# First attention: the high and low parts of the heads, written to one place each and copied to the second by GpSimd

## The chip, the cores and the metric

The kernel runs on one core of one Trainium2 chip. The metric is device time in microseconds (us), the median over runs of the whole program; before the change it is 892.95 us (three runs, 891.64 to 893.69).

## The reference

The program is a chain of four blocks, each with a residual and a layernorm behind it: polynomial attention, a gated FFN, softmax attention with a relative bias, and a mixture of eight experts with a shared expert. The change lies in the first attention, on x of 8 batches x 256 tokens x 256:

```python
proj = x @ w_qkv
q, k, v = jnp.split(proj, 3, axis=-1)          # 16 heads of 16 columns each
q = apply_rope(q, cos, sin); k = apply_rope(k, cos, sin)
q = layernorm(q, ln_scale, ln_bias)            # over the 16 columns of a head
k = layernorm(k, ln_scale, ln_bias)
a = jnp.einsum('bhnd,bhmd->bhnm', q, k) ** 4
a = jnp.tril(a)
denom = jnp.sum(a, axis=-1, keepdims=True)
out = jnp.einsum('bhnm,bhmd->bhnd', a / denom, v)
out = out.transpose(0, 2, 1, 3).reshape(b, n, e) @ w_out
```

## The kernel before

**Precision.** fp32 values go through TensorE as two numbers of the narrower type fp32r: a high part and a low part (value minus high part). A weight product takes three matmuls (`product3`, L443 to L445). For the scores of the first attention the parts are stacked along the contraction instead: a head of 16 columns takes four places of 16, that is 64 rows. Q stands there as high, low, high, low and K as high, high, low, low, so that one matmul over 64 rows sums all four products. The two buffers are `QS` and `KS` (tokens on partitions, per token 16 heads x 4 places x 16 columns); TensorE turns them with transposes (`heads`, L666 to L678) and ScalarE copies the turned pieces to `QT` and `KTT`, from which `scores` (L729, L730) reads.

**Loops.** The first layer runs over i = 0 to 7 batches and, in each, over p = 0 to 7 pairs of heads. One (i, p) is a slot. Every engine has its own program, written out by hand in that order, and runs it strictly in order; semaphores join them. For i = 0 and 1 the slots are the narrow ones (attention only); from i = 2 (`LAG1`) the FFN of batch i - 2 runs in the same slots (`gate_up`, `down` on TensorE, `silu`, `hidden_hi` on ScalarE, `product`, `hidden_lo` on VectorE).

**A pair of heads.** Scores on TensorE, square on ScalarE (L1405), causal mask on GpSimd (`masks`, L2529, two instructions), second square on VectorE (L1949) or ScalarE (L1388), `mix` on TensorE (L747).

**The heads of batch i + 1** are made during the slots of batch i: rope, centring, variance, scale and bias on VectorE (L1890 to L1930), which leaves the normalised heads in `SQ`. Then ScalarE writes the high parts (`head_hi_parts`, L1366 to L1375): for each half of the heads (8 heads) and for Q and K it casts the same 128x256 piece twice, to the two places that hold the high part. VectorE writes the low parts (`lo_parts`, L1932 to L1941), again twice each. One half of the heads is called a part. Then come the transposes: `heads(i+1, 0)` and `heads(i+1, 1)` read only the heads of part 0, `heads(i+1, 2)` and `heads(i+1, 3)` those of part 1. From i = 2 TensorE's slot (i, 6) is: scores, `gate_up`, `project` (the output projection of the batch before), `heads(i+1, 0)`, `down`; for i = 0 and 1 `heads(i+1, 0)` is in slot (i, 7). Batch 0 is made ahead of the first slot.

**GpSimd** in the first layer: two mask instructions per slot; in the slots of i = 2 one low part of an FFN weight tile (`raw_lo`, L2481, 128x768) behind the masks; behind the masks of (i, 6) the reciprocal deviation of the layernorm of the batch before (L2497, L2500), for which VectorE waits in slot (i, 7) (L1780).

Of the kernel before, what the change touches and what calls it, by code (L numbers as in the profile page):

```python
# [22 lines left out]
ALU = mybir.AluOpType  # L23
ACT = mybir.ActivationFunctionType
F32 = mybir.dt.float32
# [15 lines left out]
H0, D0 = 16, 16  # L41
# [46 lines left out]
def program(nc, x, rope, ln, aw0, wu1, aw2, rel, wu3, router, sel, out):  # L88
    with ExitStack() as ctx:
# [62 lines left out]
        QS = RT[:, 4096:6144]  # L152
        KS = RT[:, 6144:8192]
# [173 lines left out]
        def sems(name, phases=range(4)):  # L327
# [14 lines left out]
        split_hi = sems("split_hi", (0, 2))  # L342
        split_ready = sems("split_ready", (0, 2))
# [19 lines left out]
                 "prob_shifted probT_taken mixed2 ident_ready fixed_ready consts aw0_raw aw0_raw_rest aw0_hi aw0_ready vp_ones "  # L363
                 "rel_loaded rel_step diag_row diag_ready skewed first_normed bias_turned "
                 "bias_ready router_loaded router_hi router_ready raw_ready raw_free split_w_hi split_w passed "
                 "xo_ready var_ready eps_added rstd_ready filler_ready filled rows_in consts3 logits_done margin_ready tanh_ready mask_ready rstd_step "
                 "prefix_ready slots_ready meta_second xg_turned xg_hi xg_ready gu_done sgr_ready h_ready h_turned hg_hi "
                 "hg_ready yo_done y_scaled row_squares x_combined ffn_step ffn_rstd ffn_out").split()
        (in_step, route_step, rope_added, cen_squared, head_std, squared, masked, quartic_even, quartic_odd, mixed0, biased_ready, prob_ready, probT_turned,
         prob_shifted, probT_taken, mixed2, ident_ready, fixed_ready, consts, aw0_raw, aw0_raw_rest, aw0_hi, aw0_ready, vp_ones,  # L370
         rel_loaded, rel_step, diag_row, diag_ready, skewed, first_normed, bias_turned,
         bias_ready, router_loaded, router_hi, router_ready, raw_ready, raw_free, split_w_hi, split_w, passed,
         xo_ready, var_ready, eps_added, rstd_ready, filler_ready, filled, rows_in, consts3, logits_done, margin_ready, tanh_ready, mask_ready, rstd_step,
         prefix_ready, slots_ready, meta_second, xg_turned, xg_hi, xg_ready, gu_done, sgr_ready, h_ready, h_turned, hg_hi,
# [74 lines left out]
        def _(sp):  # L449
# [50 lines left out]
            for j in range(2, RAW1):  # L500
                raw_load(j)
            sp.wait_ge(diag_ready, 1)
            sp.dma_start(ediag, diagonals).then_inc(skewed, 16)
# [128 lines left out]
        def _(pe):  # L632
# [80 lines left out]
            def first_layer():  # L713
# [80 lines left out]
                def dense(i, p):  # L794
# [9 lines left out]
                    if p == 1:  # L804
                        if i >= LAG1:
                            pe.wait_ge(xt_ready[1], i - LAG1 + 1)
                        pe.wait_ge(split_ready[0], 8 * (i + 1))
                        heads(0, i, 2)
# [26 lines left out]
                    if p == (7 if i < LAG1 else 6) and left:  # L835
                        heads_out(0, i, 4)
                        if i:
                            pe.wait_ge(ct_ready[0], i)
                        pe.wait_ge(split_ready[0], 8 * (i + 1) + 4)
                        heads(0, i + 1, 0)  # L840
# [38 lines left out]
                for t in range(2):  # L879
                    qk(0, 1, t)  # L880
                pe.wait_ge(split_ready[0], 4)
                heads(0, 0, 0)
# [427 lines left out]
        def _(act):  # L1310
# [37 lines left out]
            def first_layer():  # L1348
# [17 lines left out]
                def head_hi_parts(b):  # L1366

                    act.wait_ge(in_step, IN_STEPS * b + 13)
                    n5 = SQ.rearrange("p (t w h d) -> p t w h d", t=2, w=2, h=H0)
                    for g in range(2):  # L1370
                        of = slice(H0 // 2 * g, H0 // 2 * (g + 1))
                        for w, (dst, places) in enumerate(((QS, (0, 2)), (KS, (0, 1)))):
                            d5 = dst.rearrange("p (t h s d) -> p t h s d", t=2, h=H0, s=4)
                            for s in places:
                                act.copy(d5[:, :, of, s, :], n5[:, :, w, of]).then_inc(split_hi[0], 1)  # L1375

# [366 lines left out]
        def _(dve):  # L1743
# [109 lines left out]
            def first_layer():  # L1853
# [12 lines left out]
                def diagonal():  # L1866

                    dve.wait_ge(diag_row, 1)
                    lo = S - MAXPOS
                    dve.tensor_copy(diagonals[:, lo:lo + TABLE], ps[0:1, 0, 0:TABLE])  # L1870
                    dve.tensor_copy(diagonals[:, 0:lo], ps[0:1, 0, 0:1].to_broadcast([1, lo]))
                    dve.tensor_copy(diagonals[:, lo + TABLE:ROWS], ps[0:1, 0, TABLE - 1:TABLE].to_broadcast([1, ROWS - lo - TABLE])
                                    ).then_inc(diag_ready, 1)

# [57 lines left out]
                def lo_parts(b, part):  # L1932

                    n5 = SQ.rearrange("p (t w h d) -> p t w h d", t=2, w=2, h=H0)
                    of = slice(H0 // 2 * part, H0 // 2 * (part + 1))
                    for w, (dst, places) in enumerate(((QS, (1, 3)), (KS, (2, 3)))):
                        d5 = dst.rearrange("p (t h s d) -> p t h s d", t=2, h=H0, s=4)
                        dve.wait_ge(split_hi[0], 8 * b + 4 * part + 2 * w + 2)
                        for s in places:
                            dve.tensor_tensor(d5[:, :, of, s, :], n5[:, :, w, of], d5[:, :, of, 0, :].bitcast(F32), ALU.subtract  # L1940
                                              ).then_inc(split_ready[0], 1)  # L1941

# [27 lines left out]
                def narrow_slot(i, p):  # L1970
# [29 lines left out]
                    if p == 7:  # L2000
                        if i:
                            norm(0, i - 1, 2, xr_a, X1[(i - 1) % 2])
                        dve.wait_ge(split_ready[0], 8 * (i + 2))
                        rope_half(i + 2, 0)
                        if not i:
                            rope_half(i + 2, 1)
# [74 lines left out]
                for g in range(2):  # L2081
                    lo_parts(0, g)
                dve.wait_ge(split_ready[0], 8)
                for t in range(2):
# [378 lines left out]
        def _(pool):  # L2463
# [60 lines left out]
            def masks(i, p):  # L2524
# [6 lines left out]
                m.then_inc(masked, 1)  # L2531

            aw = AW[:].rearrange("p a b c -> p a (b c)")
            n = iterations[0]
            pool.wait_ge(bias_ready, 1)
            pool.wait_ge(aw0_ready, 3)
            pool.memset(filler[:, :, 0:E + 1], 0.0).then_inc(filler_ready, 1)
            pool.iota(filler[:, :, E + 1:ROW].bitcast(I32), [[P, FILLERS], [0, 1]], 2 * T, 1).then_inc(filler_ready, 1)
            for i in range(n):
                for p in range(H0 // 2):  # L2540
                    masks(i, p)
                    for j in range(TILES1):
                        ahead = H0 // 2 * (i - LAG1) + p + 1 - j
                        if ahead == 1:
                            raw_lo(j)
                    if p == 3 and i > LAG1:
                        x1_rstd(i - LAG1 - 1)
                    if p == 6 and i:
                        layernorm_rstd(0, i - 1, 2)
                    if p == 4 and i == n - 2:  # L2550
                        pool.wait_ge(qk_ready[0], 2 * n)
                        aw2_part(0)
                    if p == 1 and i == n - 1:
                        aw2_part(1)
# [201 lines left out]
```

## Time and profile before

| | |
|---|---|
| runs | 892.95 us median, 891.64 to 893.69 |
| the profiled execution, its own time | 892.41 us |
| its span, first to last instruction | 890.7 us |
| TensorE (PE) busy, 7136 matmuls | 817.4 us, 92% |
| VectorE (DVE) busy | 651.1 us, 73% |
| ScalarE (ACT) busy | 580.2 us, 65% |
| GpSimd (POOL) busy | 437.9 us, 49% |

The first layer takes roughly the first 380 us of the span. The page is read in this order: the busy times, the share of each engine in the chain that ended last, and then the timeline of the four engines where the heads of a batch are split. In the timeline an instruction's row gives its start, its duration (for a merged row that of all xN together), and in brackets how long its engine had been idle before it and whose instruction released it. Times are of one execution.

### The profile page before, as it was taken

Reading aid. Unit: us, or ns where it says so; the run is one execution under the profiler, and the core shown is the slowest. Engines: PE = TensorE matmul, PEld = TensorE weight load, DVE = VectorE, ACT = ScalarE, POOL = GpSimd, SP = SyncE. Lnnn points to the kernel's source line nnn. Section 1 sums busy time; section 2 is a strip of 40 time slices with the busy share of each in tenths; the row PEclk is TensorE's granted clock in tenths of the full one; section 3 lists DMA queues with packets and bytes.
Section 4 is the critical chain, followed back from the end, with each engine's and each line's share of the span. In section 5 each row is a group of like instructions: output and inputs, shape, how many; then the busy total and the mean of one; then the engine's idle time right before and its main releaser. Section 6 shows DMA issues by size and latency. Waiting matters only on the chain.

```text
span 890.7 us, 20883 instructions
## 1 busy us (share of the span) xinstructions
PE 817.4 (92%) x7136; PEld 689.0 (77%) x7136; DVE 651.1 (73%) x2050; ACT 580.2 (65%) x1230; POOL 437.9 (49%) x733
## 2 busy tenths in 40 slices
PE   3877989999999999799999999999998999899994
PEld 2555878888888899666877777777767888899984
DVE  6978789889895554788888898989886453365447
ACT  3778958677685533678778777787765223366646
POOL 0345642323254220576766767676763457244423
PEclk9989999999999999899999999999999899999998
DMA  7101220210000010101020120201013122344444
GB/s 214 55 19 42 79 84 13 84 48 1 26 24 25 26 48 13 54 22 30 23 62 27 50 66 22 54 22 42 22 58 126 41 72 84 83 130 123 125 145 180
DMA packets 54761, 54.86 MB, mean 62 GB/s; under 512 B 17953, under 2 KB 48929, under 8 KB 54658
## 3 DMA queue, kind: packets, MB, share of 16 engines
q1 hardware_dynamic: 51250, 44.18, 17.0%
q0 software_dynamic: 3408, 9.34, 3.0%
q8 instruction: 60, 0.98, 0.4%
q14 instruction: 43, 0.35, 0.1%
HBM read 32.85 MB, written 20.65 MB: 60 GB/s over the span
## 4 chain that ended last, share of the span: by engine, by line
PE 62%; DVE 14%; ACT 8%; issue 7%; POOL 6%; DMA 3%; SPq 0%; DVEq 0%; ACTq 0%; POOLq 0%
PE ps L443 12%; PE ps L445 11%; PE ps L444 11%; PE ps L978 10%; PE ps L989 5%; POOL xs L2648 3%; DVE G L2145 3%; PE ps L963 2%; PE ps L676 2%; PE ps L747 2%; DVE wu_rows L2145 2%; PE ps L948 2%; ACT G L1573 1%; PE ps L729 1%; PE ps L1199 1%
## 5 line engine op out<-in xcount | busy, mean ns | idle before, releaser
L2529 POOL TENSOR_SCALAR_AFFINE_SELECT G<-G 128x256 f32<-128x256 f32 x128 | 77.7, 631 | 134.2 <-ACT G L1405 134.1
L1573 ACT ACTIVATE G<-ps 128x512 f32<-128x512 f32 x184 | 102.9, 602 | 41.6 <-PE ps L978 40.0
L443 PE MATMUL ps<-WU 128*128 128x256 f32 x384 | 116.9, 304 | 11.4 <-DVE wu_rows L1961 5.8
L2584 POOL TENSOR_SCALAR G<-G,small 128x256 f32<-128x256 f32 x214 | 100.2, 484 | 48.9 <-DVE small L2145 47.2
L2145 DVE CUSTOM_DVE_ANT_0 G<-ps,nb 128x256 f32<-128x256 f32 x296 | 108.3, 420 | 10.7 <-PE ps L963 9.4
L444 PE MATMUL ps<-WU 128*128 128x256 f32 x384 | 108.9, 283 | 0.0
L445 PE MATMUL ps<-WU 128*128 128x256 f32 x384 | 108.7, 283 | 0.0
L2584 POOL TENSOR_SCALAR wu_rows<-wu_rows,small 128x256 f32<-128x256 f32 x154 | 72.0, 483 | 37.4 <-DVE small L2145 36.3
L978 PE MATMUL ps<-ident,G 128*128 128x128 f32 x592 | 85.2, 282 | 2.2 <-ACT G L1573 2.2
L443 PEld LDWEIGHTS ps<-WU 128*128 128x128 f32 x384 | 73.2, 191 | 18.1 <-issue 7.9
L2145 DVE CUSTOM_DVE_ANT_0 wu_rows<-ps,nb 128x256 f32<-128x256 f32 x216 | 79.6, 420 | 7.9 <-PE ps L963 6.7
L978 PEld LDWEIGHTS ps<-ident,G 128*128 128x128 f32 x592 | 65.4, 143 | 14.4 <-issue 5.8
L444 PEld LDWEIGHTS ps<-WU 128*128 128x128 f32 x384 | 73.6, 192 | 0.4
L445 PEld LDWEIGHTS ps<-WU 128*128 128x128 f32 x384 | 73.5, 191 | 0.0
L1405 ACT ACTIVATE G<-ps 128x768 f32<-128x768 f32 x64 | 52.4, 819 | 31.1 <-PE ps L730 30.6
L2687 POOL DMA_INDIRECT yy<-G x39 | 37.5, 962 | 58.4 <-ACT G L1674 58.4
L989 PE MATMUL ps<-G 128*18 128x256 f32 x1024 | 63.1, 381 | 3.0 <-ACT G L1573 2.9
L978 PE MATMUL ps<-ident,wu_rows 128*128 128x128 f32 x432 | 61.6, 278 | 1.6 <-ACT G L1573 1.6
L978 PEld LDWEIGHTS ps<-ident,wu_rows 128*128 128x128 f32 x432 | 46.8, 140 | 10.1 <-issue 3.9
L443 PE MATMUL ps<-AW,RT 128*128 128x512 f32 (+1 forms) x128 | 49.3, 385 | 5.3 <-DVE AW L1858 4.0
L1417 ACT ACTIVATE wu_rows<-ps 128x256 f32<-128x256 f32 x64 | 24.6, 384 | 43.9 <-PE ps L445 43.7
L1320 ACT CAST RT<-ps 128x512 fp32r<-128x512 f32 x64 | 37.8, 590 | 19.3 <-PE ps L676 14.5
(260 smaller groups left out, 2392.4 us busy)
## 6 DMA issues: line engine op xcount, KB each, us to landing
xs<-G SPq DMA_DIRECT2D x8, 645.0 KB, 6.4
G<-xs SPq DMA_DIRECT2D x39, 128.0 KB
G<-x SPq DMA_DIRECT2D x17, 256.0 KB, 3.1
G<-in_x SPq DMA_DIRECT2D x16, 256.0 KB, 2.8
wu_rows<-yy SPq DMA_DIRECT2D x8, 512.0 KB, 7.2
x<-G SPq DMA_DIRECT2D x15, 256.0 KB, 2.2
wu_rows<-in_wu SPq DMA_DIRECT2D x8, 384.0 KB, 5.5
wraw<-in_wu SPq DMA_DIRECT2D x8, 256.0 KB, 2.7
```

Source lines behind the costliest of these rows:

```text
L443: pe.matmul(o, lh, rh, start=start, stop=False, skip_group_check=True)
L444: pe.matmul(o, lh, rl, start=False, stop=False, skip_group_check=True)
L445: return pe.matmul(o, ll, rh, start=False, stop=stop, skip_group_check=True)
L978: m = pe.transpose(ps[:, 2 + n % 2, S * kt + P * t:S * kt + P * (t + 1)], prob(n)[:, t, P * kt:P * (kt + 1)], ident[:])
L989: m = pe.matmul(ps[32 * j:32 * j + TWO, SHARED_BANK, 0:S], vp2[:, kt, at:at + TWO], probT(h)[:, kt, :], start=half == 0 and kt == 0, stop= ...
L1320: act.copy(QT[:, 2 * n:2 * n + 2, :], halves(B_QT[f])).then_inc(heads_q[f], 1)
L1405: act.square(U(p), ps[:, b:b + 2, 0:384]).then_inc(squared, 1)
L1573: act.activation(probT(n), halves(2 + n % 2), ACT.Exp).then_inc(probT_taken, 1)
L2145: m = dve.tensor_tensor_reduce(prob(n)[:, t, :], ps[:, SCORE_BANKS[n % 4], S * t:S * (t + 1)], nbv[:, t, :], 1.0, -FMIN, ALU.add, ALU.min, ...
L2529: m = pool.affine_select(out=u, in_=u, compare_op=ALU.is_ge, fill=0.0, base=0, pattern=[[0, 2], [1, P]], channel_multiplier=-1)
L2584: m = pool.tensor_scalar(p, p, -1.0, mneg[:, k:k + 1], ALU.mult, ALU.add)
L2687: pool.indirect_dma_start(yy, bass.IndirectOffsetOnAxis(ap=at, axis=0), yo[i % 3], None).then_inc(y_sent[i % 3], 16)
```

## The change

ScalarE casts each high part once, to the first of its places, and VectorE computes each low part once, to the second place of Q and of K; Q keeps its layout and that of K becomes high, low, low, high (the four products are the same). GpSimd gets a new step `second_places(b, part)`: two copies for Q (one per token tile, 8 heads x 32 columns, places 2 and 3 from places 0 and 1) and two for K (place 2 from place 1, place 3 from place 0), each 128x256. It waits for the low parts of its half of the heads, and counts a new semaphore `split_copied`, for which the transposes now wait instead of `split_ready`. The step stands ahead of the first slot for batch 0, and behind the masks of (i, 6) and (i, 7) for the two parts of batch i + 1; in (i, 6) it stands ahead of the layernorm's reciprocal deviation. A semaphore of the bias set-up (`diag_ready`) is folded into another to make room for the new one.

```diff
@@ TensorE
-                        pe.wait_ge(split_ready[0], 8 * (i + 1))
+                        pe.wait_ge(split_copied, 2 * (i + 1))
                         heads(0, i, 2)
...
-                        pe.wait_ge(split_ready[0], 8 * (i + 1) + 4)
+                        pe.wait_ge(split_copied, 2 * (i + 1) + 1)
                         heads(0, i + 1, 0)
...
-                pe.wait_ge(split_ready[0], 4)
+                pe.wait_ge(split_copied, 1)
                 heads(0, 0, 0)
@@ ScalarE, head_hi_parts
-                        for w, (dst, places) in enumerate(((QS, (0, 2)), (KS, (0, 1)))):
+                        for w, dst in enumerate((QS, KS)):
                             d5 = dst.rearrange("p (t h s d) -> p t h s d", t=2, h=H0, s=4)
-                            for s in places:
-                                act.copy(d5[:, :, of, s, :], n5[:, :, w, of]).then_inc(split_hi[0], 1)
+                            act.copy(d5[:, :, of, 0, :], n5[:, :, w, of]).then_inc(split_hi[0], 1)
@@ VectorE, lo_parts
-                    for w, (dst, places) in enumerate(((QS, (1, 3)), (KS, (2, 3)))):
+                    for w, dst in enumerate((QS, KS)):
                         d5 = dst.rearrange("p (t h s d) -> p t h s d", t=2, h=H0, s=4)
-                        dve.wait_ge(split_hi[0], 8 * b + 4 * part + 2 * w + 2)
-                        for s in places:
-                            dve.tensor_tensor(d5[:, :, of, s, :], n5[:, :, w, of], d5[:, :, of, 0, :].bitcast(F32), ALU.subtract
-                                              ).then_inc(split_ready[0], 1)
+                        dve.wait_ge(split_hi[0], 4 * b + 2 * part + w + 1)
+                        dve.tensor_tensor(d5[:, :, of, 1, :], n5[:, :, w, of], d5[:, :, of, 0, :].bitcast(F32), ALU.subtract
+                                          ).then_inc(split_ready[0], 1)
@@ GpSimd
+            def second_places(b, part):
+
+                of = slice(H0 // 2 * part, H0 // 2 * (part + 1))
+                q5, k5 = (d.rearrange("p (t h s d) -> p t h s d", t=2, h=H0, s=4) for d in (QS, KS))
+                pool.wait_ge(split_ready[0], 4 * b + 2 * part + 2)
+                for t in range(2):
+                    pool.tensor_copy(q5[:, t, of, 2:4, :], q5[:, t, of, 0:2, :])
+                pool.tensor_copy(k5[:, :, of, 2, :], k5[:, :, of, 1, :])
+                pool.tensor_copy(k5[:, :, of, 3, :], k5[:, :, of, 0, :]).then_inc(split_copied, 1)
...
             pool.memset(filler[:, :, 0:E + 1], 0.0).then_inc(filler_ready, 1)
+            for part in range(2):
+                second_places(0, part)
             pool.iota(filler[:, :, E + 1:ROW].bitcast(I32), [[P, FILLERS], [0, 1]], 2 * T, 1).then_inc(filler_ready, 1)
...
                     if p == 3 and i > LAG1:
                         x1_rstd(i - LAG1 - 1)
+                    if p >= 6 and i < n - 1:
+                        second_places(i + 1, p - 6)
                     if p == 6 and i:
                         layernorm_rstd(0, i - 1, 2)
```

GpSimd's program around slots (2, 6) to (3, 2), where batch 3 is handed on, before (L2481 is `raw_lo`, L2529 the masks, L2497 and L2500 the reciprocal deviation):

```order
L2529 AFFINE_SELECT G<-G 128x2x128 x2
L2481 TENSOR_TENSOR WU<-wu_rows,WU 128x768
L2497 TENSOR_SCALAR small<-small 128x2
L2500 TENSOR_TENSOR small<-small 128x2
L2529 AFFINE_SELECT G<-G 128x2x128 x2
L2481 TENSOR_TENSOR WU<-wu_rows,WU 128x768
L2529 AFFINE_SELECT G<-G 128x2x128 x8
```

and after (lines of the changed file; L2537 to L2539 are the copies of `second_places`):

```order
L2527 AFFINE_SELECT G<-G 128x2x128 x2
L2479 TENSOR_TENSOR WU<-wu_rows,WU 128x768
L2537 COPY RT<-RT 128x8x32 x2
L2538 COPY RT<-RT 128x2x8x16
L2539 COPY RT<-RT 128x2x8x16
L2495 TENSOR_SCALAR small<-small 128x2
L2498 TENSOR_TENSOR small<-small 128x2
L2527 AFFINE_SELECT G<-G 128x2x128 x2
L2479 TENSOR_TENSOR WU<-wu_rows,WU 128x768
L2537 COPY RT<-RT 128x8x32 x2
L2538 COPY RT<-RT 128x2x8x16
L2539 COPY RT<-RT 128x2x8x16
```

Four copies have come in behind the masks and the weight part of each of the two slots; in slot (2, 6) they stand ahead of the reciprocal deviation. From i = 3 on the same holds without the weight part.

At the start of the program GpSimd had, after the memset of the filler rows, only the iota before the first masks:

```order
L2473 MEMSET G 128x640
L2537 MEMSET G 128x5x257
L2538 IOTA G 128x5
L2529 AFFINE_SELECT G<-G 128x2x128 x30
L2497 TENSOR_SCALAR small<-small 128x2
```

and now has the copies of both parts of batch 0 behind that memset:

```order
L2471 MEMSET G 128x640
L2545 MEMSET G 128x5x257
L2537 COPY RT<-RT 128x8x32 x2
L2538 COPY RT<-RT 128x2x8x16
L2539 COPY RT<-RT 128x2x8x16
L2537 COPY RT<-RT 128x8x32 x2
L2538 COPY RT<-RT 128x2x8x16
L2539 COPY RT<-RT 128x2x8x16
L2548 IOTA G 128x5
```

The copies of part 0, for which TensorE's first transposes wait, come behind a memset that has nothing to do with them.

## Rows read from the trace of the kernel before

**Rows 1.** stretches: busy us by engine (x instructions), clock, DMA, GB/s.
```profile
30.00:85.00 55.00, 41.47 (x350) 31.50 (x352) 45.55 (x73) 44.30 (x78) 27.04 (x38) 0.91 0.15 46
125.00:162.50 37.50, 36.93 (x329) 32.59 (x328) 32.80 (x64) 28.19 (x56) 11.63 (x20) 1.00 0.14 42
```

**Rows 2.** one line's instructions: duration ns min/median/max, first and last start.
```profile
L1375 ACT CAST RT<-G x64: 400/407/411, 25.4 to 262.9; 128x256 fp32r<-128x256 f32 x64
...
L1940 DVE TENSOR_TENSOR RT<-G,RT x64: 409/417/2036, 26.2 to 265.9; 128x256 fp32r<-128x256 f32 x64
```

**Rows 3.** the timeline of GpSimd: start us, us, line, what, [idle before <-releaser].
```profile
26.19 1.18 POOL L2537 MEMSET G<- 128x1285 f32 x1 [23.49 <-DVE nb L2080]
48.88 1.76 POOL L2529 TENSOR_SCALAR_AFFINE_SELECT G<-G 128x256 f32<-128x256 f32 x2 [2.74 <-ACT G L1405]
55.45 0.77 POOL L2529 TENSOR_SCALAR_AFFINE_SELECT G<-G 128x256 f32<-128x256 f32 x2 [4.81 <-ACT G L1405]
...
276.66 0.60 POOL L2476 CAST AW<-wraw 128x512 fp32r<-128x512 f32 x1
```

**Rows 4.** the timeline at batch 0, of VectorE and of TensorE.
```profile
26.19 2.77 DVE L1940 TENSOR_TENSOR RT<-G,RT 128x256 fp32r<-128x256 f32 x8
...
32.40 0.96 DVE L1949 TENSOR_TENSOR ring<-G 128x768 f32<-128x768 f32 x1 [0.78 <-POOL G L2529]
...
27.75 1.03 PE L676 MATMUL ps<-ident,RT 128*128 128x128 f32 x8
```

**Rows 5.** the timeline at batch 1, of VectorE and of TensorE.
```profile
46.37 2.77 DVE L1940 TENSOR_TENSOR RT<-G,RT 128x256 fp32r<-128x256 f32 x8 [0.85 <-ACT RT L1375]
49.05 0.95 DVE L1949 TENSOR_TENSOR ring<-G 128x768 f32<-128x768 f32 x1
...
54.18 0.69 DVE L1890 TENSOR_TENSOR G<-ps,ropet 128x512 f32<-128x512 f32 x1 [2.91 <-PE ps L445]
...
47.94 3.73 PE L676 MATMUL ps<-ident,RT 128*128 128x128 f32 x16 [1.62 <-DVE RT L1940]
```

**Rows 6.** the timeline at batch 2, of VectorE and of TensorE.
```profile
72.68 2.77 DVE L1940 TENSOR_TENSOR RT<-G,RT 128x256 fp32r<-128x256 f32 x8 [0.85 <-ACT RT L1375]
...
79.01 0.90 DVE L1780 TENSOR_SCALAR G<-G,small 128x256 f32<-128x256 f32 x2 [0.94 <-POOL small L2500]
...
74.99 1.09 PE L676 MATMUL ps<-ident,RT 128*128 128x128 f32 x8
...
80.06 0.63 PE L791 MATMUL ps<-ident,G 128*128 128x128 f32 x4 [0.82 <-DVE G L1780]
81.23 0.50 PE L443 MATMUL ps<-AW,RT 128*128 128x512 f32 x1 [0.54 <-DVE G L1893]
```

**Rows 7.** the timeline at batch 3, of GpSimd and of TensorE.
```profile
110.88 0.95 POOL L2529 TENSOR_SCALAR_AFFINE_SELECT G<-G 128x256 f32<-128x256 f32 x2 [3.21 <-ACT G L1405]
111.80 1.99 POOL L2481 TENSOR_TENSOR WU<-wu_rows,WU 128x768 fp32r<-128x768 f32 x1
...
110.70 1.03 PE L676 MATMUL ps<-ident,RT 128*128 128x128 f32 x8
...
115.22 0.45 PE L443 MATMUL ps<-WU 128*128 128x256 f32 x1 [2.25 <-DVE wu_rows L1961]
```

**Rows 8.** the timeline at batches 4 and 7, of ScalarE, GpSimd and TensorE.
```profile
148.10 2.56 ACT L1375 CAST RT<-G 128x256 fp32r<-128x256 f32 x8
150.55 0.81 ACT L1405 ACTIVATE G<-ps 128x768 f32<-128x768 f32 x1
...
151.43 1.01 POOL L2529 TENSOR_SCALAR_AFFINE_SELECT G<-G 128x256 f32<-128x256 f32 x2 [4.12 <-ACT G L1405]
...
152.14 1.03 PE L676 MATMUL ps<-ident,RT 128*128 128x128 f32 x8
...
264.06 0.95 POOL L2529 TENSOR_SCALAR_AFFINE_SELECT G<-G 128x256 f32<-128x256 f32 x2 [3.10 <-ACT G L1405]
...
264.21 1.03 PE L676 MATMUL ps<-ident,RT 128*128 128x128 f32 x8
```

More of the change, by code:

```diff
@@ L363, in program @@
                  "prob_shifted probT_taken mixed2 ident_ready fixed_ready consts aw0_raw aw0_raw_rest aw0_hi aw0_ready vp_ones "
-                 "rel_loaded rel_step diag_row diag_ready skewed first_normed bias_turned "
+                 "rel_loaded rel_step diag_row skewed first_normed bias_turned "
                  "bias_ready router_loaded router_hi router_ready raw_ready raw_free split_w_hi split_w passed "
-                 "xo_ready var_ready eps_added rstd_ready filler_ready filled rows_in consts3 logits_done margin_ready tanh_ready mask_ready rstd_step "
+                 "split_copied xo_ready var_ready eps_added rstd_ready filler_ready filled rows_in consts3 logits_done margin_ready tanh_ready mask_ready rstd_step "
                  "prefix_ready slots_ready meta_second xg_turned xg_hi xg_ready gu_done sgr_ready h_ready h_turned hg_hi "
@@ L370, in program @@
          prob_shifted, probT_taken, mixed2, ident_ready, fixed_ready, consts, aw0_raw, aw0_raw_rest, aw0_hi, aw0_ready, vp_ones,
-         rel_loaded, rel_step, diag_row, diag_ready, skewed, first_normed, bias_turned,
+         rel_loaded, rel_step, diag_row, skewed, first_normed, bias_turned,
          bias_ready, router_loaded, router_hi, router_ready, raw_ready, raw_free, split_w_hi, split_w, passed,
-         xo_ready, var_ready, eps_added, rstd_ready, filler_ready, filled, rows_in, consts3, logits_done, margin_ready, tanh_ready, mask_ready, rstd_step,
+         split_copied, xo_ready, var_ready, eps_added, rstd_ready, filler_ready, filled, rows_in, consts3, logits_done, margin_ready, tanh_ready, mask_ready, rstd_step,
          prefix_ready, slots_ready, meta_second, xg_turned, xg_hi, xg_ready, gu_done, sgr_ready, h_ready, h_turned, hg_hi,
@@ L501, in _ @@
                 raw_load(j)
-            sp.wait_ge(diag_ready, 1)
+            sp.wait_ge(rel_step, 3)
             sp.dma_start(ediag, diagonals).then_inc(skewed, 16)
@@ L1872, in diagonal @@
                     dve.tensor_copy(diagonals[:, lo + TABLE:ROWS], ps[0:1, 0, TABLE - 1:TABLE].to_broadcast([1, ROWS - lo - TABLE])
-                                    ).then_inc(diag_ready, 1)
+                                    ).then_inc(rel_step, 1)
                 dve.wait_ge(consts, 32)
@@ L2002, in narrow_slot @@
                             norm(0, i - 1, 2, xr_a, X1[(i - 1) % 2])
-                        dve.wait_ge(split_ready[0], 8 * (i + 2))
+                        dve.wait_ge(split_ready[0], 4 * (i + 2))
                         rope_half(i + 2, 0)
@@ L2082, in first_layer @@
                     lo_parts(0, g)
-                dve.wait_ge(split_ready[0], 8)
+                dve.wait_ge(split_ready[0], 4)
                 for t in range(2):
```

## The prediction

> **What bounds the kernel now.** I read the busy times first: TensorE is busy for 92% of the span, GpSimd for half of it. A whole-program share says nothing about one stage, so next come the stretches of the first layer [rows 1]. In 125 to 162.5 us, one full batch in the steady state, TensorE is busy for 36.93 of 37.5 us at the full clock, VectorE for 32.80, ScalarE for 28.19. Nothing that is taken off VectorE or ScalarE there can shorten the batch by more than the 0.57 us that TensorE idles; anything that makes TensorE wait lengthens it. In 30 to 85 us, with attention alone, TensorE is busy for 41.47 of 55 us, VectorE for 45.55 and ScalarE for 44.30: here VectorE, strictly in order, sets much of the pace, and work taken off it may count. Last come the timelines of all engines at the moment when TensorE asks for the new heads, `heads(b, 0)`, for each batch b. The question is: what ends last there, now and after the change?
>
> **What is removed.** ScalarE casts 8 pieces per batch at 0.407 us each by the row, VectorE subtracts 8 at 0.417 us [rows 2]. Back to back they overlap: eight take 2.56 us on ScalarE [rows 8] and 2.77 us on VectorE [rows 4 to 6], so 0.31 and 0.35 us apiece. Four of each go: 1.25 us of ScalarE and 1.4 us of VectorE per batch, 10 and 11 us over eight batches. VectorE also starts after one cast and not after two, 0.35 us sooner.
>
> **What is added.** GpSimd makes four copies of 128x256 per half batch, and TensorE waits for them. No such copy is in the trace. The nearest rows: two masks of the same 128x256 take 0.77 us undisturbed, a cast of 512 columns 0.60 us, a memset of 1285 columns 1.18 us [rows 3]. The memset gives 0.9 ns a column, so half a 512 cast is at least 0.30 us, and the mask gives 0.39. I take 0.39 us, 1.55 us for four; the lower end is 1.2 us for four. The upper end comes from a mask pair that took 1.76 us, where VectorE ran a square from two SBUF operands (49.05, 0.95 us) at the same time [rows 3, 5]: 0.77 + 0.95 is 1.72. So GpSimd stood while VectorE worked. At that rate, 0.88 us each, four copies take 3.5 us. Between these ends I add, batch by batch, only the VectorE instructions of two SBUF operands that stand beside the copies: the two low parts of the other half (0.7 us), and a square where one follows.
>
> The Trainium skill says, in "SBUF — State Buffer", section "Who interferes with whom", that a VectorE instruction with two SBUF inputs and a GpSimd instruction that reads SBUF share one read interface, and that the second to come waits for the whole of the first. The trace agrees (1.76 against 0.77 us). By that rule in its strictest form, with every copy behind one low part, half a batch would cost 1.55 + 4 x 0.35 = 2.95 us; by the uncontended row it would be 1.55. It speaks against this change in particular, since the copies are released just as VectorE goes on to the other half.
>
> **Batch 0.** Before, TensorE began the heads at 27.75, just behind VectorE's first low parts. Now GpSimd first runs the memset of the filler rows (26.19 to 27.37 [rows 3]), then four copies: 27.37 + 1.55 = 28.9, with a little overlap of the last low parts 29.05. VectorE's first square waited for that chain (idle 0.78 until the mask came [rows 4]), and from there VectorE runs without a real gap, so the delay passes on whole: +1.3 us (1.2 to 2.5). The 1.4 us that VectorE saves here only lengthen that wait.
>
> **Batch 1.** Relative to the shifted start, VectorE's low parts begin at 46.37 - 0.35 = 46.02 and half are done at 46.7; the copies run beside 0.7 us of low parts and the square of 0.95 us [rows 5]: done between 46.7 + 1.55 = 48.25 and 49.9. TensorE began at 47.94. It is late by 0.3 to 2.0; since the square follows at once I take +1.5. VectorE gains nothing by being early: it already idled 2.91 us for TensorE's product behind these heads.
>
> **Batch 2.** Here VectorE does set the pace: 2.77 us of low parts, then residual, statistics and GpSimd's deviation, then the norm at 79.01, for which TensorE idled 0.82 us, and a rope for which it idled 0.54 [rows 6]. VectorE comes 1.7 us sooner. The rope needs a product that TensorE makes behind the heads, which start at about the old time (half of the low parts at 73.05, copies to 74.6 or 75.3, against 74.99). So TensorE gets back at most 0.82 + 0.54 = 1.36, and -0.7 is my value (-1.4 to +0.3).
>
> **Batch 3** (handed on in i = 2). Its copies stand behind the masks and the 128x768 weight part. ScalarE's square comes 1.25 us sooner, so the masks start at 109.65 and not at 110.88, take 0.95, the weight part 1.99 [rows 7], the copies 1.55: 114.1. TensorE wanted them at 110.70, so it stalls 3.4 us. But it had 110.70 + 2.27 us of work and then 2.25 us of idle time before 115.22, waiting for VectorE's product, which is now earlier. 114.1 + 2.27 = 116.4 against 115.22: +1.2 us (0.9 to 2.0).
>
> **Batches 4 to 7**, the pattern of the steady state. The casts on ScalarE end at 150.55 less 1.25 = 149.3, so the masks go from 151.43 to 150.2 and end at 151.0. The low parts of the first half are ready before that. Copies: 151.0 + 1.55 = 152.55, beside the low parts of the second half 153.25. TensorE began at 152.14 [rows 8]. Stall 0.4 to 1.1, with one more two-operand instruction beside them 1.6; I take 1.1. Batches 5 and 6 repeat this within 0.1 us. In batch 7 the masks come later against TensorE (264.06 against 264.21): 264.06 - 1.25 + 0.8 + 2.25 = 265.9, a stall of 1.7. Together 5.0 us (2.1 to 7.5), against 0.57 us of idle time per batch to hide it in, and that idle time stands ahead of the heads, so it hides none. The second half of each batch is copied behind the masks of (i, 7) and wanted a slot later: hidden. The deviation behind the copies is asked for by VectorE's statistics only after they are done: hidden. Behind slot (6, 7) nothing of the change is left, and the delay goes to the end, since every later block hangs on the first layer's output.
>
> **The sum.** 1.3 + 1.5 - 0.7 + 1.2 + 5.0 = +8.3 us. The profiled execution took 892.41 us, so 900.7; the median of the runs is 892.95, half a microsecond above it, which is inside their spread. I forecast 900.7. The ends of the terms add to +3.1 (1.2 + 0.3 - 1.4 + 0.9 + 2.1) and +14.3; they do not all fall on one side, so the case's own range is 895.5 to 905.5.
>
> **The rivals.**
> - *The copies are in time, and the relief of VectorE counts: not slower.* It decides at the point where four copies take less than 152.14 - 151.0 = 1.1 us, 0.28 us each; from there on the steady state is unchanged. At that point batch 0 costs 27.37 + 1.1 - 27.75 = 0.7, batch 1 nothing (46.7 + 1.1 is 47.8), batch 2 gives back 1.4, batch 3 costs 109.65 + 0.95 + 1.99 + 1.1 + 2.27 - 115.22 = 0.7: 892.4. At 0.20 us each it is 0.3 us less at batches 0, 1 and 3 each: 891.5. Should batch 1's wait of 1.62 us for the low parts [rows 5] and the 2.25 us of batch 3 go as well, it would be under 889. For it: VectorE's load in the stretch to 85 us, and the half of a 512 cast at 0.30. Against: the mask row at 0.39, and the order, which puts masks and weight part ahead of the copies. Chance 7%, of which 3% for the last form.
> - *The stalls are taken back later.* TensorE's stalls let ScalarE and VectorE run ahead, and waits behind them shrink; if most of 8 us went so, the time would stay at 893. Against it: one wait of half a microsecond in a steady batch, ahead of the heads. Chance 5%.
> - *Full contention.* Each copy waits for one VectorE instruction and takes 0.88 us: 3.5 us for four. Then batch 0 costs 3.1 (27.37 + 3.5), batch 1 2.4, batch 3 3.1, and each of the four last 2.4 to 3.1: 10.5. With -0.3 for batch 2 the sum is 18.8 us: 911. For it: the 1.76 us row. Against: VectorE has only two or three such instructions beside the copies. [...] Chance 13%.
> - The forecast's own case: 75%.
>
> **Range and chances.** The range to hold the time 8 times in 10 is 895 to 906.5: nearly all of the first case and a part of the full contention. A change under 0.2% (1.8 us) is about what a measurement of this kernel can't tell from none. Faster by more: 3% (the last form of the first rival); within: 9% (the rest of it, and the second rival); slower by more: 88%.
>
> **What would show it.** In the profile after: the copies in GpSimd's rows, 0.39 us each undisturbed, a merged four taking 1.55 to 2.3; `heads(b, 0)` on TensorE with an idle time before it released by GpSimd, about 1 us at batches 4 to 6, more at 7, 3.4 at 3; the steady batch a little above 38.5 us and not 37.5; VectorE's first square at 33.7. GpSimd's busy time up by 64 copies (eight for each of eight batches) at 0.39 us and more, 25 to 35 us. It is wrong if TensorE's transposes stand without a wait on the copies, or if the steady batch keeps its 37.5 us.

## The result and the profile after

The changed kernel took 897.54 us in the median (895.04 to 899.14, 9 runs) against 892.87 us (888.77 to 893.69, 9 runs) of the kernel before on the same chip: a ratio of 1.0060, with a 95% interval of 1.0047 to 1.0072. It is slower, by 4.7 us between the medians. Its profiled execution took 899.14 us with a span of 897.4 us, so 6.7 us more span than before; it was the slowest of the nine, 1.6 us above their median. A second set of runs is among the experiments (ratio 1.0085).

The page's busy times, share of the span, instructions:

```profile
PE 816.7 (91%) x7136; PEld 687.8 (77%) x7136; DVE 645.2 (72%) x2018; ACT 569.8 (63%) x1198; POOL 462.3 (52%) x797
```

ScalarE lost 10.4 us of busy time and VectorE 5.9 us (before: 580.2 and 651.1), GpSimd gained 24.4 (437.9), and TensorE, the engine that sets the end, has the same work to do and waits more. What it waits for in 18 to 300 us is in the table of waits (engine, what it waited for; us in total, times, longest):

```profile
PE ps L676 <- POOL RT L2539: 12.4, 8, 3.4
...
PE ps L443 <- POOL WU L2479: 3.4, 4, 1.7
...
PE ps L443 <- DVE wu_rows L1959: 2.2, 5, 0.5
```

Line 676 is the transposes of the heads, line 2539 the last copy of `second_places`: eight waits, one for each batch, and none of them stood in the trace before. They replace the one of 1.62 us for VectorE's low parts at batch 1 [rows 5] and the one of 2.25 us for `wu_rows` in batch 3 [rows 7]. The eight, as TensorE's timeline has them; batches 0 to 3 answer to [rows 4], [rows 5], [rows 6] and [rows 7], batches 4 and 7 to [rows 8]:

```profile
29.05 1.10 PE L676 MATMUL ps<-ident,RT 128*128 128x128 f32 x8 [0.89 <-POOL RT L2539]
51.02 3.65 PE L676 MATMUL ps<-ident,RT 128*128 128x128 f32 x16 [2.74 <-POOL RT L2539]
76.99 1.06 PE L676 MATMUL ps<-ident,RT 128*128 128x128 f32 x8 [1.48 <-POOL RT L2539]
116.90 1.94 PE L676 MATMUL ps<-ident,RT 128*128 128x128 f32 x8 [3.38 <-POOL RT L2539]
158.08 1.06 PE L676 MATMUL ps<-ident,RT 128*128 128x128 f32 x8 [0.88 <-POOL RT L2539]
196.62 1.07 PE L676 MATMUL ps<-ident,RT 128*128 128x128 f32 x8 [0.88 <-POOL RT L2539]
235.17 1.06 PE L676 MATMUL ps<-ident,RT 128*128 128x128 f32 x8 [0.88 <-POOL RT L2539]
273.61 1.06 PE L676 MATMUL ps<-ident,RT 128*128 128x128 f32 x8 [1.32 <-POOL RT L2539]
```

From 158.08 to 196.62 it is 38.54 us, and 38.55 to the next: the steady batch has grown from 37.5 to 38.5. GpSimd's own timeline shows what each wait consists of, here at batches 0, 1, 3 and 4 (they answer to [rows 3, 7, 8]):

```profile
26.43 1.17 POOL L2545 MEMSET G<- 128x1285 f32 x1 [23.73 <-DVE nb L2078]
27.55 0.76 POOL L2537 CAST RT<-RT 128x256 fp32r<-128x256 f32 x2
28.25 0.40 POOL L2538 CAST RT<-RT 128x256 fp32r<-128x256 f32 x1
28.60 0.40 POOL L2539 CAST RT<-RT 128x256 fp32r<-128x256 f32 x1
...
48.40 1.07 POOL L2537 CAST RT<-RT 128x256 fp32r<-128x256 f32 x2 [0.74 <-DVE RT L1938]
49.41 1.12 POOL L2538 CAST RT<-RT 128x256 fp32r<-128x256 f32 x1
50.48 0.40 POOL L2539 CAST RT<-RT 128x256 fp32r<-128x256 f32 x1
...
112.30 0.95 POOL L2527 TENSOR_SCALAR_AFFINE_SELECT G<-G 128x256 f32<-128x256 f32 x2 [1.97 <-ACT G L1404]
113.22 1.97 POOL L2479 TENSOR_TENSOR WU<-wu_rows,WU 128x768 fp32r<-128x768 f32 x1
115.13 0.93 POOL L2537 CAST RT<-RT 128x256 fp32r<-128x256 f32 x2
116.01 0.40 POOL L2538 CAST RT<-RT 128x256 fp32r<-128x256 f32 x1
116.36 0.40 POOL L2539 CAST RT<-RT 128x256 fp32r<-128x256 f32 x1
...
155.11 0.81 POOL L2527 TENSOR_SCALAR_AFFINE_SELECT G<-G 128x256 f32<-128x256 f32 x2 [2.90 <-ACT G L1404]
155.88 0.98 POOL L2537 CAST RT<-RT 128x256 fp32r<-128x256 f32 x2
156.82 0.59 POOL L2538 CAST RT<-RT 128x256 fp32r<-128x256 f32 x1
157.35 0.58 POOL L2539 CAST RT<-RT 128x256 fp32r<-128x256 f32 x1
```

At batch 3 TensorE stood ready at 116.90 - 3.38 = 113.52, when the masks were over (113.25); the weight part and then the copies kept it to 116.90. At batch 4 it was ready at 157.20, and the copies ended at 157.93, right behind masks that end at 155.92. One line's copies (minimum, median, maximum in ns; first and last start):

```profile
L2538 POOL CAST RT<-RT x16: 394/396/1119, 28.3 to 278.4; 128x256 fp32r<-128x256 f32 x16
```

How the delay grows is read by setting the same instruction of the two timelines side by side: TensorE's transposes at the end of a batch's slots 6 and 7 (its first product after the rope at batch 2). Each cell is a start, and the last column what the batch added.

| batch | before | after | later by | added |
|---|---|---|---|---|
| 0, heads | 27.75 | 29.05 | 1.3 | +1.3 |
| 1 | 57.05 | 58.95 | 1.9 | +0.6 |
| 2 | 81.23 | 83.91 | 2.7 | +0.8 |
| 3 | 119.10 | 124.01 | 4.9 | +2.2 |
| 4 | 156.62 | 162.57 | 5.95 | +1.0 |
| 5 | 194.26 | 201.11 | 6.85 | +0.9 |
| 6 | 231.75 | 239.67 | 7.9 | +1.1 |
| 7 | 269.17 | 278.11 | 8.9 | +1.0 |

The whole delay is there by the last hand-over. The same comparison on VectorE's statistics gives +8.7 at 300 us and still at 358 us, +7.9 from 560 to 687 us; in the expert block it falls to +6.8.

### The profile page after: what moved, and what is told of

Read it like the earlier page. It is cut to its first block, busy times and chain, and to the rows that moved or that the text cites. A ratio compares the mean times of both kernels' runs of the same rounds, so it can differ in the third digit from the quotient of the medians.

```text
span 897.4 us, 20883 instructions
## 1 busy us (share of the span) xinstructions
PE 816.7 (91%) x7136; PEld 687.8 (77%) x7136; DVE 645.2 (72%) x2018; ACT 569.8 (63%) x1198; POOL 462.3 (52%) x797
## 4 chain that ended last, share of the span: by engine, by line
PE 63%; DVE 14%; POOL 8%; ACT 7%; issue 6%; DMA 2%; DVEq 0%; SPq 0%; ACTq 0%; POOLq 0%
PE ps L443 12%; PE ps L445 11%; PE ps L444 11%; PE ps L978 9%; PE ps L989 5%; PE ps L676 3%; POOL xs L2660 3%; DVE G L2143 3%; PE ps L963 2%; PE ps L747 2%; DVE wu_rows L2143 2%; PE ps L948 1%; PE ps L729 1%; ACT G L1572 1%; POOL G L2527 1%
## 5 line engine op out<-in xcount | busy, mean ns | idle before, releaser
L1320 ACT CAST RT<-ps 128x512 fp32r<-128x512 f32 x64 | 37.7, 589 | 37.5 <-PE ps L676 32.7
L676 PE MATMUL ps<-ident,RT 128*128 128x128 f32 x272 | 39.8, 294 | 15.1 <-POOL RT L2539 12.4
```

Of the source, the lines that this page charges most:

```text
L676: m = pe.transpose(ps[:, bank, S * g + P * t:S * g + P * (t + 1)], w[:, t, 2 * n + g, :], ident[:])
L1320: act.copy(QT[:, 2 * n:2 * n + 2, :], halves(B_QT[f])).then_inc(heads_q[f], 1)
```

## The experiments

Each kernel was run in five rounds against the kernel before. The first four shared one set of runs of before (median 890.72 us), the last four another (892.72 us); between the two sets only ratios are compared. "Later by" is the start of the same VectorE statistics in the profiled executions, less that of before. It contains how early the first layer starts in that execution: VectorE's first low parts start at 26.19 us before, at 25.44 in the last row, at 26.82 in the first, and in between in the others.

| kernel | ratio to before | later by at 300 us | at the end |
|---|---|---|---|
| after, again | 1.0085 [1.0060, 1.0109] | +8.9 | +7.0 |
| layout only | 1.0009 [0.9992, 1.0026] | -0.3 | -0.4 |
| relief only | 0.9917 [0.9893, 0.9940] | -4.8 | -6.4 |
| copies first | 0.9997 [0.9981, 1.0012] | +0.1 | -1.9 |
| memset late | 1.0088 [1.0073, 1.0103] | +6.4 | +4.9 |
| copies before the weight part | 1.0034 [1.0021, 1.0047] | +5.7 | +3.0 |
| copies first, from batch 2 on | 0.9965 [0.9948, 0.9982] | -1.5 | -4.4 |
| copies first, batches 2, 3, 7 | 0.9966 [0.9955, 0.9977] | -3.6 | -5.8 |

**The changed kernel again**, unchanged, as the measure for the other three of its set.

> The changed kernel again, for a second profile. Theory A (what the first layer loses stays lost, the later blocks differ by chance): the delay is about 8 us at the end of the second attention (the last layernorm statistics there, 695.6 us in the first profile after against 687.8 before), as in the first profile, and the difference of the ends lies anywhere from 5 to 9 us, with other clock grants in the expert block. Theory B (the expert block gives 2 us back whenever the first layer is late): the gain of about 2.5 us between 690 and 710 us appears again at the same place. Time 896 to 899.

898.72 us (6 runs). TensorE waits 13.1 us in 8 waits for the copies. This ratio is higher than the first set's 1.0060, but the intervals overlap. The gain in the expert block comes again at the same place: the delay of 8.2 us at 687 us is 5.75 us at TensorE's product in line 1190 (717.56 against 711.81), and 7.0 at the end.

**Layout only**: the new order of places and the new semaphore arithmetic are kept, but GpSimd copies nothing, and ScalarE and VectorE write both places in every batch, as before.

```diff
-                            act.copy(d5[:, :, of, 0, :], n5[:, :, w, of]).then_inc(split_hi[0], 1)
+                            m = act.copy(d5[:, :, of, 0, :], n5[:, :, w, of])
+                            if b not in BY_POOL:           # BY_POOL = ()
+                                m = act.copy(d5[:, :, of, 2 + w, :], n5[:, :, w, of])
+                            m.then_inc(split_hi[0], 1)
...
+                        for at in (1,) if b in BY_POOL else (1, 3 - w):
```

> The new layout of K and the new semaphore counts (one count per pair of writes, not one per write), but ScalarE and VectorE write both places as before and GpSimd copies nothing. Theory A: the time of before within 0.2% (891 to 894). If the layout or the counting cost something, it would be over 895.

Equal to before (891.95 us), and within 0.4 us of it wherever VectorE's statistics were compared. The other layout of K and the folded semaphore cost nothing that shows; the delay is in who makes the second places and when.

**Relief only**: the second places are set to zero once at the start, GpSimd copies nothing, TensorE waits for the low parts. The products with the second places are therefore left out of the result, though TensorE runs the same matmuls.

```diff
-                pool.wait_ge(split_ready[0], 4 * b + 2 * part + 2)
+                return
...
-                        pe.wait_ge(split_copied, 2 * (i + 1))
+                        pe.wait_ge(split_ready[0], 4 * (i + 1))
```

> ScalarE and VectorE write one place each and nothing is copied: the second places stay zero, so the cross products of high and low parts are left out; TensorE waits for the low parts alone. It prices the relief. By the forecast's steps: batch 0 nothing or 0.3 us, batch 1 up to 1.2 (TensorE had waited 1.62 us for the low parts), batch 2 1.4 us, batch 3 1.5 to 2.2 us, batches 4 to 7 nothing: 4 to 6 us less than before, 887 to 889. Rival (the relief is hidden everywhere): 892 to 893. The difference to the changed kernel is the price of the hand-over, 8 to 13 us.

883.98 us. Against before the relief of the two engines gains 6.7 us (890.72 - 883.98), 4.8 of them in the first layer; against the changed kernel the hand-over costs 898.72 - 883.98 = 14.7 us. The change was therefore not a copy's price on top of nothing: it bought some 7 us of relief for some 15 us of hand-over; both are above what was expected (4 to 6, and 8 to 13). Of its waits for the low or copied parts only one is left:

```profile
48.12 1.07 PE L676 MATMUL ps<-ident,RT 128*128 128x128 f32 x8 [0.64 <-DVE RT L1938]
```

**Copies first**: the same copies of batch i + 1, those of part 0 ahead of the masks of slot 6 and not behind them; those of part 1 stay behind the masks of slot 7, but come ahead of the weight part that follows there in slot (2, 7). Batch 0 is as in the change.

```diff
                 for p in range(H0 // 2):
+                    if p == 6 and i < n - 1:
+                        second_places(i + 1, 0)
                     masks(i, p)
+                    if p == 7 and i < n - 1:
+                        second_places(i + 1, 1)
...
-                    if p >= 6 and i < n - 1:
-                        second_places(i + 1, p - 6)
```

> The copies of part 0 stand ahead of the masks (and of the weight part) of slot (i, 6), and not behind them. Theory A (TensorE waits because of the order on GpSimd): the waits for the copies at batches 4 to 7 (0.9, 0.9, 0.9, 1.3 us) and 3.4 us at batch 3 go; batches 0 and 1 keep theirs (1.3 and about 1.5 us). About 5 us less than the changed kernel, 892 to 894, the same as before within 0.2%. Rival (it is the length of the copies under contention): the copies now stand beside more VectorE work and the waits stay at half or more; 895 or more.

890.79 us, the time of before, and 7.9 us less than the changed kernel on the same chip. TensorE's waits for the copies fall from 13.1 to 5.3 us, of which 2.15 and 2.46 us at batches 0 and 1, none at 2, 3 and 7, and 0.2 us in each of 4 to 6. The first row here is TensorE's wait at batch 4, the others GpSimd's timeline for it:

```profile
152.02 1.06 PE L676 MATMUL ps<-ident,RT 128*128 128x128 f32 x8 [0.22 <-POOL RT L2539]
```

```profile
149.89 0.92 POOL L2537 CAST RT<-RT 128x256 fp32r<-128x256 f32 x2 [3.07 <-DVE RT L1938]
150.75 0.59 POOL L2538 CAST RT<-RT 128x256 fp32r<-128x256 f32 x1
151.29 0.59 POOL L2539 CAST RT<-RT 128x256 fp32r<-128x256 f32 x1
151.83 0.94 POOL L2527 TENSOR_SCALAR_AFFINE_SELECT G<-G 128x256 f32<-128x256 f32 x2
```

The copies take as long as in the changed kernel (0.92, 0.59, 0.59 against 0.98, 0.59, 0.58), and GpSimd had idled 3.07 us before them. So more than half of the hand-over's 14.7 us was the place in GpSimd's program, not the copies' own time. The masks of slot 6 now come behind the copies, and TensorE has no wait for them. What was moved behind copies in slot (2, 7) does cost: there GpSimd makes the four copies from 118.81 to 120.30 and the weight part only then, until 122.07, and TensorE has a wait that it has neither before nor in the change. The row of its table for the weight parts grows from 3.4 us in the change to 5.0:

```profile
122.12 0.38 PE L443 MATMUL ps<-WU 128*128 128x256 f32 x1 [1.51 <-POOL WU L2479]
```

```profile
PE ps L443 <- POOL WU L2479: 5.0, 5, 1.7
```

TensorE's transposes of slot (2, 7) start 2.1 us ahead of before (117.04 against 119.10), its next ones 0.5 us ahead (129.07 against 129.55). The two kernels further down that put the copies first in some batches only have the same wait of 1.51 us. The weight part ahead of these copies, with the copies of part 0 first, was not tried.

**Copies before the weight part**: behind the masks, as in the change, but ahead of `raw_lo` (called in the loop over j). It differs from the change only in slots (2, 6) and (2, 7).

```diff
                     masks(i, p)
+                    if p >= 6 and i < n - 1:
+                        second_places(i + 1, p - 6)
                     for j in range(TILES1):
...
-                    if p >= 6 and i < n - 1:
-                        second_places(i + 1, p - 6)
```

> The copies stand behind the masks as in the change, but ahead of the weight part that batch 3 has in slots (2, 6) and (2, 7). It parts the weight part's share of batch 3. Theory A: TensorE's wait at batch 3 falls from 3.4 to about 1.4 us, and the 2.25 us that it idled behind the heads before the change hide that; batch 3's cost goes from 2.2 us to nothing: 896 to 897 beside a before of 890.7 and 898.7 for the change. Waits at batches 4 to 7 stay at 0.9, 0.9, 0.9 and 1.3. Rival (the masks' time or the contention sets it): the wait stays over 2.5 us.

The ratio is 1.0034, against 1.0088 of memset late in the same set, with intervals apart. In the trace the gain lies where it should: at the end of batch 3 it is 1.9 us behind before and no longer 4.9, although its delay at batch 2 is only 0.2 us smaller:

```profile
116.52 1.06 PE L676 MATMUL ps<-ident,RT 128*128 128x128 f32 x8 [2.08 <-POOL RT L2539]
...
121.01 1.09 PE L676 MATMUL ps<-ident,RT 128*128 128x128 f32 x8
```

The wait is shorter by 1.3 us (2.08 and not the 1.4 expected: beside low parts the pair of copies takes 1.12 us), and the matmuls behind it run at the full clock (more on this below). So these 3 us are not the price of one instruction alone. Memset late, with the weight part still in the way, is 2.7 us behind before at the same place, and the changed kernel's second profile 5.2: between these two the clock moves the place by 2.5 us. What the order is worth is better read from the ratios: against the changed kernel's 1.0060 and memset late's 1.0088 it is 0.26 to 0.54%, 2.3 to 4.8 us.

**Memset late**: the memset of the filler rows behind the copies of batch 0.

```diff
-            pool.memset(filler[:, :, 0:E + 1], 0.0).then_inc(filler_ready, 1)
             for part in range(2):
                 second_places(0, part)
+            pool.memset(filler[:, :, 0:E + 1], 0.0).then_inc(filler_ready, 1)
```

> The changed kernel, with the memset of the filler rows (1.17 us) behind the copies of batch 0 and not ahead of them. Theory A (the delay of batch 0 is the memset plus the copies): the copies start when half of the low parts are done, at about 26.9 us and not 27.6, so TensorE's first heads come 0.6 to 0.7 us sooner and the time falls by as much: 898 where the changed kernel took 898.7 beside a before of 890.7. Rival (batch 0 is paid by something else): no change of the first heads.

A miss. From the start of the low parts to the heads of batch 0 it is 29.39 - 26.77 = 2.62 us, against 29.05 - 26.29 = 2.76 in the changed kernel: 0.14 us saved where 0.6 to 0.7 was expected. The memset had mostly lain beside the low parts, for which the copies wait anyway, and once they start earlier they run beside low parts themselves and the pair takes 0.96 and not 0.76 us:

```profile
27.68 0.96 POOL L2537 CAST RT<-RT 128x256 fp32r<-128x256 f32 x2 [24.99 <-DVE RT L1938]
28.59 0.40 POOL L2538 CAST RT<-RT 128x256 fp32r<-128x256 f32 x1
28.93 0.40 POOL L2539 CAST RT<-RT 128x256 fp32r<-128x256 f32 x1
```

Its ratio is 1.0088, the changed kernel's second set had 1.0085 (the first 1.0060). Its profiled execution, with 895.5 us of span 2 us shorter than the changed kernel's, was the fastest of its five and had less of the low clock told of below.

**Copies first, from batch 2 on**: as copies first, but ScalarE and VectorE write both places in batches 0 and 1, where waits of 2.15 and 2.46 us had been left. **Batches 2, 3 and 7 only**: GpSimd helps only where copies first had no wait left at all.

```diff
+        BY_POOL = (2, 3, 4, 5, 6, 7)      # the other kernel: (2, 3, 7)
...
+                if b in BY_POOL:
+                    pe.wait_ge(split_copied, copied(b) + parts)
+                else:
+                    pe.wait_ge(split_ready[0], 4 * b + 2 * parts)
```

> Batches 0 and 1 are written twice by ScalarE and VectorE as before; from batch 2 on GpSimd copies, ahead of the masks. Theory A (the narrow batches 0 and 1 lose about 2 us by the copies, batches 2 and 3 gain 3.5 in this order): 2 us less than with the copies ahead of the masks everywhere, about 888 to 889 beside a before of 890.7. Rival (the relief of batches 2 and 3 hangs on the delay before them): 890 to 891.

> GpSimd copies for batches 2, 3 and 7 alone, ahead of the masks; the others as before. Theory A: batches 4 to 6 lost 0.2 to 0.4 us each in the run with the copies first, since TensorE is the bound there: about 1 us less than with batches 2 to 7, 887 to 888.5, the fastest so far of those that compute all of it. Rival (the relief in the steady batches is worth something too): no better than batches 2 to 7.

Both beat both kernels: 887.98 and 889.49 us, ratios of 0.9965 and 0.9966 to before. TensorE's table of waits has no entry for the copies in the second; in the first it has four, together 0.9 us, of 0.2 us each at batches 2 and 4 to 6. That the second would gain another microsecond over the first is not shown: its profiled execution is 1.4 us shorter (0.9 of it stands before the first heads, 26.99 against 27.86 us), its median 1.5 us longer, the ratios are equal.

## Why the prediction was right

It forecast 900.7 us and a slower kernel; the profiled execution took 899.14 us, the median was 897.54. The direction and the mechanism held: TensorE waits for the copies at each hand-over, and the steady batch grew by a microsecond. The size is less sure than 899.14 makes it look. Against the 8.3 us forecast the medians differ by 4.7 us in this set and by 8.0 in the second (898.72 - 890.72), the two profiled executions by 6.7. Its own terms, against the table of batches above:

- **The copy**, 0.39 us each undisturbed: 0.394 to 0.396 by the row. Beside low parts a pair took 1.07 and not 0.76 us, beside a square of two SBUF operands a single one 1.12 us (49.41 to 50.53, with VectorE's square from 49.13 to 50.27). That is the contention the forecast added instruction by instruction. The Trainium skill's rule for this ("SBUF — State Buffer", "Who interferes with whom") has the second to come wait for the whole of the first; by it the copy would have ended at 50.27 + 0.39 = 50.66, and it ended at 50.53, which nearly agrees. The steady state's four in 2.05 us lie between the free 1.55 and that rule's strictest form of 2.95. GpSimd's busy time rose by 24.4 us, just under the 25 to 35 forecast.
- **Batch 0**, +1.3: measured +1.3, VectorE's first square at 33.75 (33.7 said). The reason was half wrong: the memset on top is worth 0.14 us, as its experiment showed, and it is the hand-over to another engine that costs the rest.
- **Batch 1**, +1.5: the heads came 1.8 us later against the shifted start, as forecast or a little more, but 1.1 us of it was back six products later. They took 54.34 to 55.98 us after and 51.33 to 54.08 before, near the two levels of the clock (granted 0.94 and 0.54); the forecast had taken TensorE's work as the same length.
- **Batch 2**, -0.7: the wrong sign, +0.8. The heads started where the forecast had them (74.99 + 1.9 = 76.9; 76.99), but behind the wait of 1.48 us came a stretch of low clock, and the rope had to wait 2.15 us for its product:

```profile
79.85 0.78 PE L443 MATMUL ps<-AW,RT 128*128 128x512 f32 x1
...
82.00 0.40 PE L445 MATMUL ps<-AW,RT 128*128 128x512 f32 x1
```

```profile
82.50 0.69 DVE L1889 TENSOR_TENSOR G<-ps,ropet 128x512 f32<-128x512 f32 x1 [2.15 <-PE ps L445]
```

  In memset late and in the changed kernel's second profile the wait is the same (1.47 us) and the clock stays full, and there the step comes out as forecast: in memset late it is from the heads to the rope's product 82.80 - 77.45 = 5.35 us against 81.23 - 74.99 = 6.24 before, so -0.9, and in the second profile batch 2 added -0.8. VectorE's relief is real at this batch; the low clock ate it in the one execution and not in the others.
- **Batch 3**, +1.2: the stall of 3.4 us is 3.38, and the 2.25 us of idle time behind it were used up as said. The term was mis-sized (+2.2) because the forecast let the matmuls behind the heads run as before: from the heads to the end of the row they took 124.01 - 116.90 = 7.11 us against 119.10 - 110.70 - 2.25 = 6.15. In the changed kernel's second profile this batch added 3.6 us: the granted clock was 0.72 from 104 to 110 us there (1.00 in the first), the masks started at 112.60, and what batch 2 had given back was lost again. Batches 2 and 3 together added 3.0 us in the first profile and 2.8 in the second, against 0.5 forecast.
- **Batches 4 to 7**, 1.1, 1.1, 1.1 and 1.7, together 5.0: the waits are 0.88, 0.88, 0.88 and 1.32, and the batches added 4.0 in all. ScalarE's and VectorE's relief let the masks start 2.09 us ahead of TensorE's request (157.20 - 155.11), which had 0.71 us before, and the copies took 2.05, not 2.25 us.
- **"The delay goes to the end"**: it does not go there whole. It is 8.7 us up to 358 us, falls to 7.9 by 560 us, in the second attention, and from 7.9 to 6.8 us in the expert block. Copies first and relief only gain 1.0 and 0.7 us between 358 and 560 us too, layout only 0.1; why was not tried. Two stretches of the expert block, before and after, shifted by the delay (us, then busy time by engine, clock, DMA share, GB/s):

```profile
690.00:695.00 5.00, 5.00 (x38) 5.00 (x38) 1.83 (x4) 0.96 (x3) 2.65 (x2) 0.78 0.06 13
...
705.00:710.00 5.00, 5.00 (x15) 3.87 (x14) 4.64 (x12) 0.60 (x1) 2.07 (x3) 0.58 0.18 52
```

```profile
697.90:702.90 5.00, 4.54 (x40) 4.33 (x40) 2.12 (x5) 1.17 (x2) 2.63 (x2) 1.00 0.06 15
...
712.90:717.90 5.00, 5.00 (x25) 4.17 (x24) 4.60 (x12) 1.69 (x3) 2.12 (x3) 0.96 0.20 56
```

  The granted clock is higher after, which takes the delay from 7.9 to 5.4 us at 711 us; then TensorE waits 4.6 and not 3.3 us for the tile that a DMA brings to the experts' first product, and 1.3 us are lost again:

```profile
PE ps L1199 <- DMA G<-xs: 4.6, 1, 4.6
```

  Every kernel with a moved first layer gained there on balance, 0.8 to 1.9 us, whether it arrived later than before or earlier; layout only, which moved nothing, did not. Why the clock is granted otherwise is open.

In the first layer the terms add to 8.9 us where 8.3 was forecast, because a batch 1 and a steady state that were too dear by 1.9 us stand against a batch 2 and 3 that were too cheap by 2.5. The sum was better than its parts. That is luck: errors of about 2 us in either direction cancelled, and those at batches 1 to 3 come from the clock, which the forecast's terms left alone.

Of the rivals, copies in time did not come about by faster copies, and relief counted only with the copies elsewhere in the queue: from copies first on it is what the experiments measured. Full contention, 0.88 us for each copy, was refuted by the rows. The stalls were taken back later in part, some 2 of 8.9 us. The forecast did not ask the question that turned out to be worth 8 us: whether the copies' inputs were ready earlier than the masks ahead of them.

VectorE's busy time fell by 5.9 us where the removed pieces were worth 11: the low parts went from 25.2 us for 64 to 15.6 for 32, each of them longer (mean 458 and 535 ns). With the copies gone (relief only) VectorE was busy for 642.2 us, 8.9 less than before, so of the 5.1 us that are missing the copies account for 3.0; what holds the rest was not tried.

## What to carry to other kernels

When work is handed to a less busy engine, price its place in that engine's program before its duration: the same 64 copies made the kernel 0.6 to 0.9% slower behind the masks and no slower with those of part 0 ahead of them, where GpSimd idles 3 us in a steady batch. Ask of each hand-over when its input is ready, what stands ahead of it in the queue, and who waits for that, and also what now stands behind it: the best orders here still have a new wait of 1.51 us for the weight part. And move it only in those batches where the bounding engine asks late enough, since the best version here (0.35% faster than before) leaves batches 0 and 1 as they were. And measure the relief alone, with the new work left out: it says about what the move can be worth (0.8% here) before any place is tuned.

## What the runs showed of the hardware

TensorE's granted clock behind a wait is not a fixed price. These are the stretches behind the heads of batch 3, of the changed kernel and of two variants:

```profile
116.90:120.00 3.10, 3.10 (x14) 2.92 (x14) 1.37 (x4) 1.71 (x3) 1.45 (x2) 0.50 0.00 0
```

```profile
115.80:119.00 3.20, 3.19 (x20) 2.86 (x21) 1.39 (x4) 2.17 (x4) 1.45 (x2) 0.69 0.00 0
```

```profile
116.50:120.00 3.50, 3.48 (x29) 3.29 (x30) 2.34 (x5) 2.81 (x5) 3.42 (x4) 1.00 0.00 0
```

The first stood behind 3.38 us of idle time and ran at 0.50, so at 1.2 GHz; the second (memset late) behind 3.41 us, at 0.69; the third (before the weight part) behind 2.08 us, at 1.00, so at 2.4 GHz. In the kernel before, the products behind the heads of batch 3 stood behind 2.25 us and had 0.57 in 115 to 119 us. At batch 2, behind 1.47 or 1.48 us, the stretch of 5 us had 0.66 in the changed kernel and 0.68 before the weight part, but 1.00 in its second profile and in memset late. So the same wait came out with and without a low clock in two profiled executions of one kernel; this is about 1.6 us at batch 2. It did not reach the end: the second profile, ahead at batch 2, lost as much to a low clock at 104 to 110 us, and is 8.9 us late at 300 us where the first is 8.7. Such stretches may be part of why a kernel's runs spread over 4 us; that was not tried.
